# Three key chunks of values at a time: moving the join, the shift rows, K's low halves and the context load in a cross-attention kernel

## The reference

```python
q_c = _ln(x) @ W_qc + b_qc
kv_c = _ln(context) @ W_kvc + b_kvc
k_c, v_c = jnp.split(kv_c, 2, axis=-1)
c_attn_w = jax.nn.softmax(jnp.einsum('bhqd,bhsd->bhqs', q_c, k_c) * scale, axis=-1)
c_attn_out = jnp.einsum('bhqs,bhsd->bhqd', c_attn_w, v_c)
```

## Time and profile before

| | before |
|---|---|
| median of 3 runs | 2054.8 us (2049.62 to 2060.08) |
| the profiled execution | 2058.93 us, its span 2057.1 us |
| mean granted TensorE clock | 0.872 of full speed |
| busy, share of the span | PE 82%, PEld 51%, DVE 60%, ACT 49%, POOL 21% |
| cross-attentions in the span | about 391 to 836, 992 to 1416 and 1588 to 2016 us |

### The profile page before, as it was taken

One profiled execution on the slowest core, in us unless ns is written; L12 is line 12 of the kernel. 1 busy time (PEld: TensorE's weight loads), 2 busy tenths in 40 slices (PEclk: granted clock), 3 DMA queues, 4 the chain that ended last, 5 costly groups with the idle time before them and its releaser, 6 DMA issues.

```text
span 2057.1 us, 53938 instructions
## 1 busy us (share of the span) xinstructions
PE 1695.6 (82%) x20495; PEld 1053.3 (51%) x20495; DVE 1235.9 (60%) x2433; ACT 1009.7 (49%) x1911; POOL 424.9 (21%) x611
## 2 busy tenths in 40 slices
PE   4788777698888998786698999987785988999986
PEld 3455543365555655443355555665342555555554
DVE  5455443576675776265677777761454776777752
ACT  1243322175665666242366666663231565666652
POOL 7000124033232313135033444200230000000000
PEclk9799988599898998697699999986886899999986
DMA  5011122233343332040334444420041334343310
GB/s 174 31 69 67 45 50 56 55 100 108 105 116 88 112 99 71 1 94 12 79 112 114 118 120 114 109 83 1 5 101 33 91 102 114 113 113 114 97 42 9
DMA packets 178547, 166.47 MB, mean 81 GB/s; under 512 B 67551, under 2 KB 168099, under 8 KB 178403
## 3 DMA queue, kind: packets, MB, share of 16 engines
q1 hardware_dynamic: 176818, 163.35, 28.7%
q10 hardware_dynamic: 1008, 1.05, 0.2%
q0 software_dynamic: 576, 0.02, 0.0%
HBM read 114.46 MB, written 40.08 MB: 75 GB/s over the span
## 4 chain that ended last, share of the span: by engine, by line
PE 60%; DVE 15%; ACT 10%; issue 9%; DMA 3%; SPq 2%; POOL 1%; DVEq 0%; ACTq 0%; POOLq 0%
PE PS L1125 8%; PE PS L1022 8%; PE PS L1152 7%; PE PS L1016 7%; PE PS L862 6%; PE PS L1099 5%; DVE mx L1552 5%; PE PS L1011 3%; PE PS L941 3%; DVE k_lo L1460 2%; PE PS L1227 2%; ACT q_parts L795 2%; PE PS L959 2%; DMA k_dram<-k_lo 2%; ACT cxT L720 1%
## 5 line engine op out<-in xcount | busy, mean ns | idle before, releaser
L1552 DVE TENSOR_REDUCE mx<-PS 112x1 f32<-112x500 f32 x1152 | 722.7, 673 | 252.5 <-PE PS L1099 246.3
L795 ACT ACTIVATE q_parts<-PS 125x448 f32<-125x448 f32 x1152 | 563.0, 544 | 197.9 <-PE PS L1152 195.3
L585 POOL TENSOR_SCALAR cx<-cx,norm_b 125x128 f32<-125x128 f32 x384 | 304.3, 807 | 458.2 <-DMA cx<-in_ctx 351.1
L1099 PE MATMUL PS<-k_st,q_mx 50*112 50x500 f16 x1152 | 297.3, 418 | 58.4 <-issue 24.1
L1152 PE MATMUL PS<-q_st,k_st 50*125 50x112 f16 x4608 | 269.5, 240 | 54.5 <-ACT q_parts L795 20.8
L1152 PEld LDWEIGHTS PS<-q_st,k_st 50*125 50x125 f16 x4608 | 191.5, 144 | 238.1 <-ACT q_parts L795 135.3
L1125 PE MATMUL PS<-q_parts,v_sb 125*18 125x112 f32 x9216 | 311.6, 280 | 0.0
L1125 PEld LDWEIGHTS PS<-q_parts,v_sb 125*18 125x18 f32 x9216 | 230.8, 105 | 57.4 <-issue 41.2
L1099 PEld LDWEIGHTS PS<-k_st,q_mx 50*112 50x112 f16 x1152 | 101.7, 137 | 121.9 <-DVE mx L1552 64.9
L725 ACT ACTIVATE k_hi<-PS,vec 128x500 f16<-128x500 f32 x144 | 97.6, 678 | 116.9 <-PE PS L1016 116.9
L729 ACT ACTIVATE v_sb<-PS 125x512 f32<-125x512 f32 x144 | 87.3, 606 | 128.2 <-PE PS L1022 128.1
(11 more groups left out here) (266 smaller groups left out, 2028.6 us busy)
## 6 DMA issues: line engine op xcount, KB each, us to landing
k_st<-k_dram SPq DMA_DIRECT2D x864, 62.5 KB, 2.2
cx<-in_ctx SPq DMA_DIRECT2D x56, 750.0 KB
k_dram<-k_hi SPq DMA_DIRECT2D x144, 125.0 KB, 1.8
k_dram<-k_lo SPq DMA_DIRECT2D x144, 125.0 KB, 2.0
v_sb<-in_ctx SPq DMA_DIRECT2D x8, 750.0 KB
q_mx<-q_all SPq DMA_DIRECT2D x48, 99.8 KB
q_st<-q_all SPq DMA_DIRECT2D x48, 99.8 KB
q_all<-q_dram SPq DMA_DIRECT2D x18, 196.0 KB, 6.9
```

The lines of the kernel that those rows point to most:

```text
L585: last = pool.tensor_scalar(cx[:, p, c, :], cx[:, p, c, :], norm_b[:, p, 0, c:c + 1], norm_b[:, p, 1, c:c + 1], ALU.subtract, ALU.mult)
L795: act.activation(probs[:, c % RING, u * HR:(u + 1) * HR], PS[0:KC, (2 * c + u) % SC_RING, 0:HR], ACT.Exp).then_inc(sem("exp_done"), 1)
L1099: mm(PS[0:PW, MX_BANK + u % MX_RING, 0:TK], q_mx[64 * a:64 * a + ROWS, p, k, :], k_st[64 * a:64 * a + ROWS, p, k, TK * t:TK * t + TK], sta ...
L1552: dve.tensor_reduce(mx[:, r, t:t + 1], PS[0:PW, MX_BANK + u % MX_RING, 0:TK], AX.X, ALU.max)\
```

## The change

The product with the values is made for three chunks at a time, behind chunks 4, 7 and 10 and at the end of the body (before: two at a time, behind 3, 5, 7, 9, 11 and at the end). K0 moves from slot 4 to slot 5 and V0 from slot 10 to slot 9. The join moves from bank 7 at chunk 7 to bank 4 (`JOIN_BANK`, one of the banks of the units) at chunk 11, where it waits for the reduction of 23 of the 24 units, and unit 1 of the next body waits for its division. TensorE's shift comes before V1 and three chunks of values (before: V1 and values 8 and 9 ahead of it, 10 and 11 behind). VectorE takes `k_lo` after all units of its chunk (before: after the first of them), and its shift is cut in two, with the division in between. SP issues the context load after the last `k_out` of the body. The number of matmuls, reductions, copies and DMAs is the same.

```diff
--- before.py
+++ after.py
@@ -52,11 +52,11 @@
 Q_PARTS = ((0, 2), (2, B))
 
 
-SLOT_MISC = {0: (True, 8), 1: (False, 0), 2: (False, 1), 3: (False, 2), 4: (False, 3), 6: (False, 4),
-             8: (False, 5), 10: (False, 6), 11: (False, 7)}
+SLOT_MISC = {0: (True, 8), 1: (False, 0), 2: (False, 1), 3: (False, 2), 5: (False, 3), 6: (False, 4),
+             8: (False, 5), 9: (False, 6), 11: (False, 7)}
 
 MAXES = [2, 2, 2, 2, 2, 2, 2, 3, 2, 3, 2, 0]
-PAIR_SLOT = 7
+JOIN_BANK = MX_BANK + 1
 PAIRS = B // 2
 DVE_CONSTS = 2 + HG + 5
 
@@ -481,13 +481,13 @@
                         q_scores(following)
                     if behind:
                         q_max(behind)
-                        if not (isinstance(b, int) and b + 4 >= B):
-                            load((b + 4, i + 2, p))
                         k_out(behind, 0)
                         k_in(behind, 0)
                         k_out(behind, 1)
                         k_in(behind, 1)
                         k_out(behind, 2)
+                        if not (isinstance(b, int) and b + 4 >= B):
+                            load((b + 4, i + 2, p))
 
                 pipeline(sp, first, attend)
 
@@ -794,7 +794,7 @@
                             act.wait_ge(sem("scores_ready"), 2 * n + u + 1)
                             act.activation(probs[:, c % RING, u * HR:(u + 1) * HR],
                                            PS[0:KC, (2 * c + u) % SC_RING, 0:HR], ACT.Exp).then_inc(sem("exp_done"), 1)
-                    if behind:
+                    if C - 1 in SLOT_MISC and behind:
                         misc(behind, SLOT_MISC[C - 1][1])
                     if following:
                         shift_rows(following)
@@ -1084,10 +1084,12 @@
 
                 misc = preparation(layer)
 
-                def unit(batch, u):
+                def unit(batch, u, joined=None):
 
                     b, i, p = batch
                     n = n0 + b
+                    if joined is not None and u == 1:
+                        pe.wait_ge(sem("attn_out"), PAIRS * cr["n"] + joined)
                     t, a, k = u // NP, u % 2, u % NP // 2
                     if u == 0:
                         pe.wait_ge(sem(f"q_mx_loaded{p}"), 16 * (B // 2 * cr["n"] + i + 1))
@@ -1127,15 +1129,14 @@
                                   skip_group_check=True)
                     last.then_inc(sem("pv_done"), 1)
 
-                def join_pair(i, behind):
+                def join_pair(i, following):
 
                     pe.wait_ge(sem("attn_read"), n0 + 2 * i + 2)
-                    if behind:
-                        pe.wait_ge(sem("k_hi_done"), NT * (n0 + behind[0]) + 2)
-                        pe.wait_ge(sem("k_lo_done"), NT * (n0 + behind[0]) + 2)
+                    if following:
+                        pe.wait_ge(sem("max_done"), UNITS * (n0 + following[0] + 1) - 1)
                     for k, rows in enumerate((to_dims, to_sums)):
                         for r in range(2):
-                            last = mm(PS[:, MISC_BANK, k * PW:k * PW + PW], rows[:, r, :],
+                            last = mm(PS[:, JOIN_BANK, k * PW:k * PW + PW], rows[:, r, :],
                                       acc[:, r, :, :].rearrange("p a t -> p (a t)"), start=(r == 0), stop=(r == 1))
                     last.then_inc(sem("pair_ready"), 1)
 
@@ -1165,26 +1166,28 @@
                     u = 0
                     start = isinstance(b, int) and b == 0
                     joins = p == 0 and not start
+                    joined = i if p == 1 and not (isinstance(b, int) and b == 1) else None
                     for c in range(C):
                         scores(batch, c)
                         for t in range(u, u + MAXES[c]) if following else ():
-                            unit(following, t)
+                            unit(following, t, joined)
                         u += MAXES[c]
-                        if c % 2 and c > 1:
-                            values(batch, c - 3)
-                            values(batch, c - 2)
-                        if joins and c == PAIR_SLOT:
-                            join_pair(i - 1, behind)
-                        if c in SLOT_MISC:
+                        if joins and c == C - 1:
+                            join_pair(i - 1, following)
+                        if c % 3 == 1 and c > 1:
+                            for k in range(c - 4, c - 1):
+                                values(batch, k)
+                        if c in SLOT_MISC and c < C - 1:
                             of_next, k = SLOT_MISC[c]
-                            if joins and k == 5:
-                                pe.wait_ge(sem("attn_out"), PAIRS * cr["n"] + i)
                             if following if of_next else behind:
                                 misc(following if of_next else behind, k)
                     if following:
                         shift(following)
-                    values(batch, C - 2)
-                    values(batch, C - 1)
+                    of_next, k = SLOT_MISC.get(C - 1, (False, None))
+                    if behind and k is not None:
+                        misc(behind, k)
+                    for k in range(C - 3, C):
+                        values(batch, k)
                     if isinstance(b, int) and b == B - 1:
                         join_pair(PAIRS - 1, None)
 
@@ -1552,10 +1555,9 @@
                     dve.tensor_reduce(mx[:, r, t:t + 1], PS[0:PW, MX_BANK + u % MX_RING, 0:TK], AX.X, ALU.max)\
                        .then_inc(sem("max_done"), 1)
 
-                def shift(batch):
-
-                    b, i, p = batch
-                    n = n0 + b
+                def shift_split(batch):
+
+                    n = n0 + batch[0]
 
                     def step(instruction, k):
                         instruction.then_inc(sem("split_chain"), 1)
@@ -1566,8 +1568,12 @@
                     step(dve.tensor_scalar(msplit[:, :, 0], mneg[:, :], -1.0, None, ALU.mult), 2)
                     dve.scalar_tensor_tensor(out=msplit[:, :, 1], in0=mneg[:, :], scalar=-1.0, in1=msplit[:, :, 0],
                                              op0=ALU.mult, op1=ALU.subtract).then_inc(sem("split_done"), 1)
+
+                def shift_rows(batch):
+
+                    b, i, p = batch
                     dve.wait_ge(sem(f"q_loaded{p}"), 16 * (B // 2 * cr["n"] + i + 1))
-                    dve.wait_ge(sem("shift_ready"), n + 1)
+                    dve.wait_ge(sem("shift_ready"), n0 + b + 1)
                     dve.tensor_copy(q_st[0:2, p, :, :].rearrange("p k n -> p (k n)"), PS[0:2, MX_BANK, 0:QUAD * PW])\
                        .then_inc(sem("shift_done"), 1)
 
@@ -1587,15 +1593,16 @@
 
                     n = PAIRS * cr["n"] + i
                     dve.wait_ge(sem("pair_ready"), n + 1)
-                    dve.reciprocal(orec[:, :], PS[:, MISC_BANK, PW:2 * PW]).then_inc(sem("orec_done"), 1)
+                    dve.reciprocal(orec[:, :], PS[:, JOIN_BANK, PW:2 * PW]).then_inc(sem("orec_done"), 1)
                     dve.wait_ge(sem("orec_done"), n + 1)
-                    dve.tensor_tensor(OALL[:, bass.ds(i * PW, PW)], PS[:, MISC_BANK, 0:PW], orec[:, :], ALU.mult)\
+                    dve.tensor_tensor(OALL[:, bass.ds(i * PW, PW)], PS[:, JOIN_BANK, 0:PW], orec[:, :], ALU.mult)\
                        .then_inc(sem("attn_out"), 1)
 
                 def first():
                     for u in range(UNITS):
                         unit((0, 0, 0), u)
-                    shift((0, 0, 0))
+                    shift_split((0, 0, 0))
+                    shift_rows((0, 0, 0))
 
                 def attend(batch, following, behind, _):
                     b, i, p = batch
@@ -1608,15 +1615,17 @@
                             unit(following, tiles.pop(0))
                         if c == 0 and not start:
                             finish((b - 1, None, 1 - p))
-                        if p == 0 and not start and c == PAIR_SLOT + 1:
-                            divide(i - 1)
+                        for t in tiles:
+                            unit(following, t)
                         of_next, k = SLOT_MISC.get(c - 1, (True, None))
                         if behind and not of_next:
                             k_low(behind, k)
-                        for t in tiles:
-                            unit(following, t)
                     if following:
-                        shift(following)
+                        shift_split(following)
+                    if p == 0 and not start:
+                        divide(i - 1)
+                    if following:
+                        shift_rows(following)
                     if isinstance(b, int) and b == B - 1:
                         finish(batch)
                         divide(PAIRS - 1)
```

## The result

The changed kernel takes 2228.7 us (median of 4 runs, 2226.6 to 2234.0) against 2057.4 for the kernel before: a ratio of 1.0825, with a 95% interval of 1.077 to 1.0881. Forecast were 2213 us, in a range of 2120 to 2290.

The account below looks back on a forecast made before the run. TensorE was taken to set the pace, its standing still to decide. The profiled 2058.9 us plus 99 for waits and gains and 59 for the clock gave 2217, less 4 for the median 2213, range 2120 to 2290.

Parts of the forecast that it names:

- K1 behind K0, K2 behind K1, V0 behind K2: TensorE at chunks 6, 7 and 9 waits for VectorE's `k_lo`: 2.0, about 0.5 and 2.5 us.
- Rival D: K chain not felt, `k_lo` done when TensorE reaches K1 and V0; only gains stand: -88 us, 1967; chance 0.04.
- Rival C: TensorE reaches chunk 6 late enough that K1's and V0's waits are halved: 2088 us; chance 0.10.
- End of the body: Around the shift: about 0.4 us wait for VectorE's split in odd bodies; about 0.2 of 0.40 us idle stays.
- The join and the division: The join's 1.98 us wait goes; next body's unit 1 and the shift copy wait for the division at no cost.
- SP and the load: Late context load costs 0; four waits for the stacked key go, -6 us.
- The body totals: Without the clock, odd bodies take 27.7 us instead of 23.6, even ones 28.3 against 26.4 clean and 27.4 measured.
- The clock: TensorE's clock falls behind 84 new K1 and V0 waits, 0.7 us each: +59 us.
- Rival A: The K chain costs what is said but the clock stays up: 2154 us; chance 0.16.
- B: Clock stays low between a body's two waits: +168 us in place of 59, about 2320; chance 0.09.
- The three chunks at a time: Chunks 0 to 5: with three chunks of values at 4, chunk 6 starts 9.85 us into the body instead of 10.0.
- Rival E: Code fetch: more loop passes have 5 us TensorE stands at body start, 6 us each, up to 2300; chance 0.06.

Follow-up runs that it names:

- experiment 1: Changed kernel with only `k_lo` back behind the first unit of its chunk, slots kept: 2056.7 us, ratio 1.0064 to the kernel before.
- experiment 2: Changed kernel with only the slots back, K0 at 4 and V0 at 10, `k_lo` still late: median 2073 us, runs 2040.4 to 2101.7.
- experiment 4: Changed kernel with only the context load back ahead of K's halves: 2219.5 us, ratio 1.0857 to the kernel before.
- experiment 7: Kernel before with only the context load moved behind the last `k_out`: 2059.9 us, ratio 0.9993 to the kernel before.
- experiment 3: Changed kernel with both the slots and the early `k_lo` restored, values still three chunks at a time: 2058.7 us, ratio 1.0046 to the kernel before.
- experiment 5: Changed kernel with old slots, early `k_lo` and values two chunks at a time: 1992.8 us, ratio 0.9751 to the kernel before.
- experiment 6: Kernel before with only the values made three chunks at a time: 2147.7 us, ratio 1.0508 to the kernel before.
- experiment 8: Experiment 5's kernel with values 8 and 9 moved behind the shift and V1: 1977.2 us, ratio 0.9623 to the kernel before.
- experiment 9: Experiment 5's kernel with `k_lo` behind all units of its chunk: 2024.3 us, ratio 0.9826 to the kernel before.

## Why the prediction was right, and where it was not

*The bound.* Right: TensorE's queue order decided, and neither VectorE nor ScalarE became the bound; both were as busy as before.

*K1 behind K0, K2 behind K1, V0 behind K2.* Predicted 2.0, 0.5 and 2.5 us, measured 2.04, 0.56 and 2.42; in sum 42 x 5.0 = 210 us predicted and 193.8 measured, since K2's wait is there in 11 bodies and not in 42. Experiments 1 and 2 each take away one of the two edits that make the waits, and most of the loss goes. Rival D, that the chain isn't felt, needed `k_lo` to end by T + 0.36; it ended at T + 2.33. Rival C, that half is absorbed, fell with the same rows.

*End of the body.* Predicted 0.4 us for the split in odd bodies and 0.2 for the copies. The copies' wait is there (0.18 us); the split's 0.41 us is that of the body shown, and only 6 bodies have such a wait at all, 2.2 us in sum.

*The join and the division.* Right: the division is waited for by nobody, and unit 1 of the next body starts on time.

*SP and the load.* Cost 0, shown in both directions (experiments 4 and 7). The waits for the stacked key, 6 us, did go in the changed kernel, but not because the load moved, as experiments 4 and 7 show: that term of the sum came true for a reason that it did not give, and what makes these waits stays open.

*The body totals.* Predicted 27.7 and 28.3 us without the clock; in layer 2 the odd bodies took 28.5 to 31.4, 29.5 in the mean, the even ones with a join 29.9 to 32.5, 30.8 in the mean. That is 1.8 and 2.5 us more, where 2 x 0.7 stood for the clock.

*The clock.* Here the forecast was right by luck. It took 0.7 us for each of 84 waits, 59 us, and -18 for what the clock had cost at the joins: +41. TensorE's busy time did grow by 41.6 us, but not by the clock alone. Its matmuls in the bodies 0 to 13, compared at the two clocks kind by kind, cost 126 us more than they would have at 2.4 GHz throughout; in the kernel before the same figure is 46 us, in experiment 1 it is 15 (estimates, worked out from the three traces). So the clock cost 80 us, not 41: the new waits nearly 1.5 us each where 0.7 was taken (the rows of the joins had said 1.0 to 1.2), against a credit of 46 where 18 was taken. What made up for it is a gain that the forecast did not have. Before, TensorE also waited for VectorE's maxima inside its chunks, and part of that lies within the busy time of the units. Behind K1, the same three and two units, before and after:

```profile
1199.25 0.85 PE L1099 MATMUL PS<-k_st,q_mx 50*112 50x500 f16 x3
1201.19 0.84 PE L1099 MATMUL PS<-k_st,q_mx 50*112 50x500 f16 x2
...
1198.15 0.58 PE L1101 MATMUL PS<-k_st,q_mx 50*112 50x500 f16 x3
1200.22 0.38 PE L1101 MATMUL PS<-k_st,q_mx 50*112 50x500 f16 x2
```

VectorE catches up during the new waits. At 2.4 GHz a unit then adds 125 ns to TensorE's busy time instead of 157, some 32 us for the 1008 units of these bodies, and the visible waits for the maxima fall from 11.9 to 2.5 us. The rule of the Trainium skill that was weighed ("TensorE: Matmul & The Clock Gate", "HAM oscillation — how this bites in real kernels") would have made the new waits' clock cost 0; 64 slow stretches at 84 waits of 2.0 to 2.4 us say otherwise. Rival A, with the clock up, and B, with it down between the waits, both fell: it fell at three waits in four and mostly came back in between.

*The three chunks at a time.* This is the step that was not seen. The working gave them -0.15 us a body, and in the changed kernel that was about right, because the new K waits let ScalarE and VectorE catch up. But rival D's -88 us, "only the gains stand", took the join's gain for what is left when the K waits go. Experiment 3 shows that it is not: +0.5%, with new waits of 1.85 us a body, where chunk 4 and chunk 10 are too long and the chunks between too short. The gain is real only with two chunks at a time (experiment 5, -2.5%), and 6 shows the price of three alone (+5%). 

*What is left.* 2229 - 2213 = 16 us, again a sum of misses on both sides. In the profiled executions the 21 odd bodies grew by 120 us (86 and 29 for the clock were predicted), the 18 even ones with a join by 48 (34 - 18 + 25), the three bodies 0 by 8 (12 + 4), the three bodies 14 by 2.5 where -9 was predicted, and the rest of the span fell by 8. In these sums are two bodies of layer 1 in which TensorE stands 5 us before the first scores, with nothing named: bodies 4 and 8 before, 36.2 and 38.7 us, bodies 4 and 10 after, 45.8 and 39.2. Their cause was not studied. Rival E, that there would be more of them, is not supported by the changed kernel, in which there are two again; other kernels here have none (experiments 1 to 5, 8), one, two or three.

## What to carry to other kernels

A step that waits for another engine to read its bank needs, between it and the step before it, more of its own work than that engine has queued ahead of the read: count the reader's instructions, here two or three reductions of 0.61 us and a copy of 0.73. Moving the read ahead of the reductions was one statement and worth 156 us; spacing the steps gave back most of it too. Group work that nobody waits for evenly along the chain of those that are waited for: the same matmuls in twos and in threes differed by 3 to 5%. And an edit should be priced also with its neighbours undone, since a large wait hides what a second edit costs. Nor is a difference of busy time the price of the clock: compare the same matmuls at the same clock first.

## What was not expected of the hardware

The granted clock doesn't answer to the length of a wait in proportion. At waits of 2.04 and 2.42 us a stretch at 1.2 GHz began in 64 of 84 cases, at waits of 1.46 and 1.25 us in 6 of 84; a wait shorter by 0.6 to 1.2 us thereby gave back more busy time than idle time, 102 us beside 84 in the profiled executions. But it isn't the single wait alone: with waits of 0.41 and 0.73 us that lie 1.4 us apart (experiment 3) the clock fell 17 times in 42 bodies, and with three of 0.57, 0.86 and 0.86 us in each body, some 4 us apart (experiment 9), it fell once, at a stand of 5.2 us. What decides between these was not found. Busy time can hold waiting: two units took 0.84 us or 0.38 at the same clock. And an idle time that is labelled "issue" can be a wait for another engine, here of a step that waits for two semaphores.
